# Sparse experts with rings of 12 row slots and 8 weight slots, weights and rows five tiles ahead, two unread products, output by quarters

## The reference

```
    x = x + ctx @ Wo
    m = _layernorm(x, ln2_g, ln2_b)
    xt = m.reshape(-1, Dd)
    probs = jax.nn.softmax(xt @ Wg, axis=-1)
    wts, idx = jax.lax.top_k(probs, K)
    wts = wts / jnp.sum(wts, axis=-1, keepdims=True)
    h1 = jax.nn.gelu(jnp.einsum('td,edf->etf', xt, W1) + b1[:, None, :])
    ye = jnp.einsum('etf,efd->etd', h1, W2) + b2[:, None, :]
    sel = ye[idx, jnp.arange(T)[:, None], :]
    moe_out = jnp.sum(wts[..., None] * sel, axis=1).reshape(Bb, Ss, Dd)
    return x + moe_out
```

## Time and profile before

| what | value |
|---|---|
| median of 3 runs | 2333.95 us |
| the profiled execution | 2350.25 us |
| its span, first to last instruction | 2348.5 us |
| TensorE busy | 1893.6 us (81%) |
| VectorE busy | 1552.4 us (66%) |
| ScalarE busy | 958.3 us (41%) |
| GpSimd busy | 748.9 us (32%) |
| mean granted TensorE clock | 0.904 |
| the expert tiles, first hidden product to last down product | 2201.33 to 2326.83 us |

### The profile page before, as it was taken

How to read it: one execution, slowest core, us unless ns; L and a number is a source line. 1 busy time by engine, 2 the same in 40 slices (tenths; PEclk the granted TensorE clock), 3 DMA queues, 4 the chain that set the end, 5 groups by cost and what they waited for, 6 DMA issues and landing times.

```text
span 2348.5 us, 50210 instructions
## 1 busy us (share of the span) xinstructions
PE 1893.6 (81%) x20232; PEld 1212.9 (52%) x20232; DVE 1552.4 (66%) x3648; ACT 958.3 (41%) x2463; POOL 748.9 (32%) x959
## 2 busy tenths in 40 slices
PE   6678999889898899976787899999999646472864
PEld 3324556555545566435575566666666213252654
DVE  5699985788846754478615766676764899766112
ACT  3436654666536322324124455555553001150232
POOL 2244554555414242134404100000002753325222
PEclk9779999999999999987798999999999877785797
DMA  9000001000071000700341010000000000210465
GB/s 381 7 1 0 1 1 67 4 5 4 4 306 59 3 1 1 293 14 2 111 148 31 19 37 19 19 19 19 10 1 1 0 9 18 102 57 30 144 193 156
DMA packets 56039, 134.80 MB, mean 57 GB/s; under 512 B 13865, under 2 KB 34044, under 8 KB 48128
## 3 DMA queue, kind: packets, MB, share of 16 engines
q1 hardware_dynamic: 52512, 125.48, 15.3%
q0 software_dynamic: 3296, 6.12, 0.8%
HBM read 112.13 MB, written 20.12 MB: 56 GB/s over the span
## 4 chain that ended last, share of the span: by engine, by line
PE 47%; DVE 29%; issue 10%; ACT 7%; DMA 4%; POOL 2%; SPq 1%; POOLq 0%; DVEq 0%; another core or an unknown queue 0%; ACTq 0%
PE PS L2442 3%; PE PS L418 3%; PE PS L362 3%; PE PS L454 3%; PE PS L3105 3%; PE PS L3095 3%; PE PS L3153 2%; DVE arena L1733 2%; DVE arena L248 2%; PE PS L2242 2%; DMA answers<-arena 2%; PE PS L3145 1%; DVE arena L3561 1%; ACT arena L3217 1%; PE PS L3137 1%
## 5 line engine op out<-in xcount | busy, mean ns | idle before, releaser
L315 POOL TENSOR_TENSOR arena<-arena 128x4 f32<-128x4 f32 (+2 forms) x101 | 115.5, 1145 | 852.1 <-DVE arena L259 415.4
L3217 ACT ACTIVATE arena<-PS,arena 128x289 f32<-128x289 f32 x256 | 127.0, 506 | 176.5 <-DVE arena L3322 173.3
L362 PE MATMUL PS<-arena 128*128 128x512 f32 x310 | 168.4, 664 | 5.0 <-DVEq L4058 4.2
L1797 POOL TENSOR_TENSOR arena<-arena 128x128 f32<-128x128 f32 x384 | 140.5, 407 | 52.7 <-PE PS L1660 29.4
L3105 PE MATMUL PS<-arena 128*128 128x289 f32 x512 | 136.1, 409 | 2.3 <-DVE arena L3316 1.7
L1733 DVE RECIPROCAL arena<-PS 128x128 f32<-128x128 f32 x96 | 91.6, 954 | 58.2 <-PE PS L1698 58.0
L1764 ACT COPY arena<-PS 32x128 f32<-32x128 f32 x384 | 99.5, 259 | 52.1 <-PE PS L1674 47.2
L1183 POOL TENSOR_TENSOR arena<-arena 128x512 f32<-128x512 f32 x64 | 85.0, 1328 | 108.7 <-DVE arena L1328 108.7
L382 PE MATMUL PS<-arena 128*128 128x128 f32 x288 | 50.0, 313 | 69.2 <-DVE arena L294 29.4
L3105 PEld LDWEIGHTS PS<-arena 128*128 128x128 f32 x512 | 92.7, 191 | 24.4 <-issue 2.9
L454 PE MATMUL PS<-arena 128*128 128x128 f32 (+4 forms) x576 | 87.6, 298 | 16.8 <-DVE arena L409 4.1
(11 more groups left out here) (411 smaller groups left out, 4844.0 us busy)
## 6 DMA issues: line engine op xcount, KB each, us to landing
arena<-in_ctx SPq DMA_DIRECT2D x48, 1090.0 KB, 7.3
arena<-in_f_w SPq DMA_DIRECT2D x39, 514.0 KB
lists<-arena SPq DMA_DIRECT2D x8, 1040.0 KB, 10.9
arena<-in_f_w SPq DMA_DIRECT2D x32, 256.0 KB
arena<-in_ctx SPq DMA_DIRECT2D x16, 512.0 KB, 4.2
arena<-in_mid SPq DMA_DIRECT2D x1, 3796.5 KB, 11.8
arena<-in_late SPq DMA_DIRECT2D x1, 3204.0 KB, 11.9
arena<-in_w SPq DMA_DIRECT2D x1, 3017.0 KB, 13.5
```

Of the source, the lines that this page charges most:

```text
L315: e.tensor_tensor(x, x, half.broadcast_to(list(x.shape)), ALU.pow).then_inc(*T.done("norm_root", tag))
L362: e.matmul(g.PS[:, b, :], g.C["ident"], g.const_words[:, 0:512], start=True, stop=True)
L1797: k = e.tensor_tensor(dst[:, b], spread(src[:, b, :], [P, HG, S], 1), spread(self.g.C["headmask"], [P, HG, S], 2), ALU.mult)
L3217: e.activation(self.weights(n, k, 0, UL), PS[:, k, 0:UL], ACT.Exp, bias=self.st[:, h, k:k + 1], accum_out=self.st[:, h, 4 + k:5 + k]).then ...
```

## The change

It touches the expert part of the last layer and the output:

- The rows get 12 slots of their own (`SLOTS`), the weights 8 (`RING`). The rows have their own events (`f3_tile`), so that `turn` waits for the rows alone and `hidden` for the weights.
- The weights of five tiles (`LEAD`) are issued before the list is complete, then the rows of these five, then weights and rows of one tile after the other.
- `weights(k)` now waits for `down(k - 8)` and `rows(k)` for the scatter of tile k - 12.
- TensorE turns all four quarters of the gates and then does all four bias products.
- Two unread products are left of 14.
- The output is written in four DMAs, each after its quarter has been added to.

```diff
@@ L3Ffn
-    RING = 6
+    RING, SLOTS, LEAD = 8, 12, 5
@@ __init__
-        self.x = [room.take(self.ROW) for _ in range(self.RING)]
+        self.x = [room.take(self.ROW) for _ in range(self.SLOTS)]
@@
     def loaded(self, k):
+        return f"f3_tile{k % self.SLOTS}", k
+
+    def weighed(self, k):
         return f"f3_weights{k % self.RING}", k
@@ sp
         def rows(k, at):
-            j = k - self.RING
+            j = k - self.SLOTS
             for w in T.due(("f3_rows_out", j), (f"f3_gathered{j % 4}", j)):
                 e.wait_ge(*w)
-            e.dma_start(self.x[k % self.RING], lists[bass.DynSlice(at, 1)].rearrange("a p w -> (a p) w")).then_inc(*T.done(*self.loaded(k), 16))
+            e.dma_start(self.x[k % self.SLOTS], lists[bass.DynSlice(at, 1)].rearrange("a p w -> (a p) w")).then_inc(*T.done(*self.loaded(k), 16))
 
         for w in T.due(("f3_list", 0)):
             e.wait_ge(*w)
-        ahead = [weights(k) for k in range(3)]
+        at = [weights(k) for k in range(self.LEAD)]
         for w in T.due(("f3_scattered", 2 * NT - 1)):
             e.wait_ge(*w)
-        for k in range(self.TILES):
-            rows(k, ahead[k] if k < 3 else weights(k))
+        for k in range(self.LEAD):
+            rows(k, at[k])
+        for k in range(self.LEAD, self.TILES):
+            rows(k, weights(k))
@@ after the loads of the answers
+        out = self.out.rearrange("b s d -> (b s) d")
+        for q in range(NQ):
+            for w in T.due(("f3_final", q)):
+                e.wait_ge(*w)
+            e.dma_start(out[QW * q:QW * q + QW, :].rearrange("(a p) d -> p a d", p=P), quarter(g.X, q)).then_inc(*T.done("out", q, 16))
@@ hidden
-            for w in T.due(free[b], ("f3_sT_dve", k)):
+            for w in T.due(free[b], self.weighed(k), ("f3_sT_dve", k)):
@@
-        idle_pe(e, T, g, free, 6, 14)
+        idle_pe(e, T, g, free, 6, 2)
@@ dve, the last additions
-                e.tensor_tensor(x, x, quarter(self.back[c], q), ALU.add).then_inc(*T.step())
+                e.tensor_tensor(x, x, quarter(self.back[c], q), ALU.add).then_inc(*(T.done("f3_final", q) if c else T.step()))
@@ sync_program
-    e.dma_start(out.rearrange("b s d -> (b s) d").rearrange("(t p) d -> p t d", p=P), g.X).then_inc(*T.done("out", 0, 16))
```

More of the change, by code:

```diff
@@ L70 @@
         "query_out": "lin_out", "located": "lin_out", "select": "cleared", "second_pool": "first",
-        "shifted": "beta", "list": "picked", "count": "picked", "end": "picked", "tiles": "picked", "past": "picked"}
+        "shifted": "beta", "list": "picked", "count": "picked", "end": "picked", "tiles": "picked", "past": "picked", "final": "residual",
+        "weights6": "rows0", "weights7": "rows1", "tile8": "v30", "tile9": "v31", "tile10": "v32", "tile11": "v33"}
+KIND.update({f"tile{k}": f"context{k}" for k in range(8)})
 def work_of(name):
@@ L3657, in weights @@
             e.dma_start(self.w[k % self.RING], t["f3_w"][bass.DynSlice(x, 1)].rearrange("a p f -> (a p) f")).then_inc(
-                *T.done(f"f3_weights{k % self.RING}", (k, 0), 16))
+                *T.done(*self.weighed(k), 16))
             return at
         def rows(k, at):
-            j = k - self.RING
+            j = k - self.SLOTS
             for w in T.due(("f3_rows_out", j), (f"f3_gathered{j % 4}", j)):
                 e.wait_ge(*w)
-            e.dma_start(self.x[k % self.RING], lists[bass.DynSlice(at, 1)].rearrange("a p w -> (a p) w")).then_inc(*T.done(*self.loaded(k), 16))
+            e.dma_start(self.x[k % self.SLOTS], lists[bass.DynSlice(at, 1)].rearrange("a p w -> (a p) w")).then_inc(*T.done(*self.loaded(k), 16))
         for w in T.due(("f3_list", 0)):
             e.wait_ge(*w)
-        ahead = [weights(k) for k in range(3)]
+        at = [weights(k) for k in range(self.LEAD)]
         for w in T.due(("f3_scattered", 2 * NT - 1)):
             e.wait_ge(*w)
-        for k in range(self.TILES):
-            rows(k, ahead[k] if k < 3 else weights(k))
+        for k in range(self.LEAD):
+            rows(k, at[k])
+        for k in range(self.LEAD, self.TILES):
+            rows(k, weights(k))
         for k in range(self.TILES - 4, self.TILES):
@@ L3742, in turn @@
                 e.wait_ge(*w)
-            e.transpose(g.PS[:, b, 0:P], self.x[k % self.RING][:, 0:D], C["ident"]).then_inc(*T.done("f3_turned", k))
+            e.transpose(g.PS[:, b, 0:P], self.x[k % self.SLOTS][:, 0:D], C["ident"]).then_inc(*T.done("f3_turned", k))
             free[b] = ("f3_sT_dve", k)
@@ L3843, in pool @@
         for k in range(self.TILES):
-            at = self.x[k % self.RING][:, D + 1:D + 2].bitcast(mybir.dt.uint32)
+            at = self.x[k % self.SLOTS][:, D + 1:D + 2].bitcast(mybir.dt.uint32)
             for w in T.due(("f3_rows_out", k)):
@@ L4026, in dve @@
                     e.wait_ge(*w)
-                e.tensor_scalar(self.y[j % 4], g.PS[:, 4 + j % 2, 0:D], self.x[j % self.RING][:, D:D + 1], None,
+                e.tensor_scalar(self.y[j % 4], g.PS[:, 4 + j % 2, 0:D], self.x[j % self.SLOTS][:, D:D + 1], None,
                                 ALU.mult).then_inc(*T.done("f3_rows_out", j))
@@ L4074, in pool_program, with sync_program @@
         e.drain().then_inc(*T.done("left_pool", x.ends))
-def sync_program(e, T, layers, g, out):
+def sync_program(e, T, layers, g):
     t = g.t
@@ L4088, in sync_program @@
         e.wait_ge(*w)
-    e.dma_start(out.rearrange("b s d -> (b s) d").rearrange("(t p) d -> p t d", p=P), g.X).then_inc(*T.done("out", 0, 16))
-    for w in T.due(("out", 0), ("in_x", 0), ("in_const", 0), ("in_weights", "first"), ("in_weights", "mid"), ("in_weights", "late"),
+    for w in T.due(*(("out", q) for q in range(NQ)), ("in_x", 0), ("in_const", 0), ("in_weights", "first"), ("in_weights", "mid"), ("in_weights", "late"),
                    ("f2_slots_in", "zero"), ("f2_slots_in", "rows"), *((f"f2_gathered{q}", 4 * q + 3) for q in range(NQ)), ("f2_scattered", NT - 1),
@@ L4099, in program @@
         layers = [x(g) for x in LAYERS]
+        layers[11].out = out
         layers[8].after, layers[9].before = layers[9], layers[8]
@@ L4108, in program @@
         pool_program(dry, View(tally, "pool"), layers)
-        sync_program(dry, View(tally, "sp"), layers, g, out)
+        sync_program(dry, View(tally, "sp"), layers, g)
         tally.dry = False
@@ L4130, in _ @@
         def _(e):
-            sync_program(e, View(tally, "sp"), layers, g, out)
+            sync_program(e, View(tally, "sp"), layers, g)
 def constants():
```

## The result

The changed kernel takes **2273.8 us** (median of 4 runs, 2270.9 to 2277.1), the kernel before 2332.0 us (median of 4). The ratio is 0.9752, with a 95% interval of 0.9728 to 0.9776: 58 us less, between 52 and 63. The forecast was 2269 with a range of 2259 to 2286. Later, on another chip, both were timed again, and the ratio was 0.9709 (0.9680 to 0.9738).

A forecast was written before the change was run, and what follows sets the result against it. The prediction took a closed loop of scatter, row load and products over three tiles as the bound, no engine being busy. Savings of 3.4 + 10.1 + 49.1 + 2.1 = 64.7 us from 2333.95 gave 2269, range 2259 to 2286.

The forecast's parts named there:

- The closed loop of three tiles: Last layer's tiles: each round of scatter, row load and products covers three tiles in 10.7 us, with TensorE waiting.
- loop term: Tiles of the last layer: with the longer rings the loop takes 76.4 us instead of 125.5, 49.1 us less.
- Clock: Start of the tiles: an early full clock saves up to 4 us, a late one loses some 2 us; nothing added.
- The DMA term: Tile loop: DMA engines need 2.14 us a tile, above TensorE's 1.90, so the step was taken as 1.95 us.
- Rival A: Tile loop: the DMA engines become the bound, steps of 2.14 to 2.4 us, time 2276 to 2286; chance 0.28.
- The weights' loop holds six and takes no longer: Weight ring: weights(k) wait for down(k - 8), done in step k - 6, so this loop takes no longer than the rows'.
- The start: Before the first tile: gates and bias products 3.4 us earlier, fewer unread products 10.1 us less, turn(0) at 2187.1.
- The output: End of the kernel: with four output DMAs only the last 256 KB is left, 2.1 us less, bounds 0 and 2.5.
- Rival B: Tile loop: the scatter queues behind the loads, steps of 3.9 us or more, slower at about 2341; chance 0.03.
- C: Tile loop: TensorE loses its clock, half-speed steps of 3.8 us, only the ends gain, 2341 at worst; chance 0.03.
- D: Tile loop: something else closes a loop of three tiles, leaving the ends' 15.6 us, time 2318; chance 0.04.
- The sum: Whole kernel: 3.4 + 10.1 + 49.1 + 2.1 = 64.7 us less, 2.8% of 2350.25, giving 2269.

The follow-up runs named there:

- rings6: The changed kernel with both rings back at 6 slots (RING = 6, SLOTS = 6): 2336.2 us, ratio 0.9940 to the kernel before on that chip.
- slots6: The changed kernel with only the row ring back at 6 slots, weights keeping 8: ratio 0.9908 to the kernel before, tiles 118.8 us.
- idle14: The changed kernel with 14 unread products instead of 2: profiled span 2278.2 us, start and tiles together 129.9 us.
- ringsonly: The changed kernel's rings and loads with the start and output of the kernel before: ratio 0.9751 to the kernel before on chip A.
- changed: The changed kernel, unaltered, run again on chip C: 2274.4 us, ratio 0.9709 to the kernel before.
- after: The changed kernel's profiled execution on the first chip: 2277.1 us, span 2275.1 us, ratio 0.9752 to the kernel before.
- moretraffic: The changed kernel with one more load of 132 KB for each tile from the sixth on: tiles 86.3 us, profiled span 2280.6 us.
- oneout: The changed kernel with one output DMA of 1024 KB instead of four: end 21.4 us, profiled span 2277.9 us.
- ringsonly2: The changed kernel's rings and loads with the start and output of the kernel before, run on chip C: 2286.4 us, ratio 0.9768.
- alternate: The changed kernel with gates and bias products in alternation as before the change: start 48.3 us, tiles 75.0 us, profiled span 2280.1 us.

## Why the prediction was right, step by step

*The closed loop of three tiles* was read rightly, and the runs show it: rings6 brings back 125.5 us, slots6 118.8.

*The size of the loop term* was right for partly wrong reasons, and so in part by luck. Forecast: 76.4 us, from 2.4 + 37 x 1.95 + 1.8. Measured: 76.5, or 76.8 to the end of the last product, as the forecast counts. It comes from 1.90 per step without any lag of the DMA engines, and some 2 us of half clock at the start, a cost that the prediction named under "Clock" and set to nothing. The 0.05 us that it added to each of 37 steps for the DMA engines is as much, and did not come. idle14 and ringsonly, whose tiles begin at full clock, have the 74.5 us that stood there as TensorE's end. The cost isn't steady: `changed`, the same program as after, had 75.2, as its clock rose 3 us earlier.

*The DMA term* was mis-sized. "2.14 us for a tile" divided the busy time of a half-loaded stretch by its tiles. At TensorE's pace the engines took in a tile every 1.90 us at a share of 0.97 (after) or 0.99 (changed), which is at most 1.84 to 1.88 us of busy time. The share in a stretch with gaps doesn't give the time at full load; it was some 15% too high. Rival A therefore fell: TensorE never waited in the tiles. How narrowly is open; the share of 0.99 speaks for little room, but moretraffic, which was to show it, ran at SP's pace. SP was the next bound in the prediction too, at 1.71 us a tile, 0.19 under TensorE's.

The Trainium skill, DMA: Bandwidth & Descriptors, section "Where 436 GB/s comes from", puts the limit from HBM at about 358 GB/s, which the prediction weighed. That was nearer to the 346 of `changed` than the 298 of the row of before; but it isn't a limit on this core, as the context loads moved 422.

*"The weights' loop holds six and takes no longer"* was wrong. The rows of a tile are issued behind its weights, so the loop closes through turn and holds RING - 3 = 5 tiles. It cost nothing only because 8 slots are just enough; with 6 it cost 22 us.

*The start*: 13.5 us forecast (3.4 + 10.1), with nothing late at turn(0). Counted from the first turned gate to the first hidden product it was 12.7 us (30.0 before, 17.3 after) and 12.5 us on chip C (29.8 and 17.4). Something was late after all: the rows, by 1.3 us in the changed kernel, because the last scatter into the lists set them and not TensorE. The prediction's margin of 4.6 us (rows at 2182.5, turn(0) at 2187.1) came out of a disturbed profile. In the profile of before the gates came 7.6 us late (36.7 against 29.1 us after the first scatter) and the last scatter only 2.5 us late (43.5 against 41.0 us), so TensorE seemed to have 5.1 us more than it has. This also puts turn(0) at 2179.3 and not near 2187. Of the two edits the products gave most: idle14's start is 9.1 us longer than oneout's on the same chip. The order of the gates gives 3.4 us where 14 products follow and nothing waits (58.9 for ringsonly2, 55.5 for idle14), 1.9 us of start beside two products, and of that 0 to 1.6 us remain after the tiles (alternate).

The first two profiles differ by 20.3 us at the start. 12.7 us of that are the change, and 7.6 us lie ahead of the gates, where in the last 14 us VectorE idles up to 2.4 us ahead of single small operations in the profile of before, and less than 0.4 us in that of after. It isn't the change's: the same kernel code has starts 11 us apart on chips A and C (69.7 and 58.9 for ringsonly and ringsonly2).

*The output*: 2.1 us forecast, 2.6 to 2.7 measured (ringsonly2 against changed; oneout, from the last addition on). The outputs landed in 2.9 us at the median, where the best row of that size had 3.0.

*Rival B* (the scatter behind the loads, slower) did not come: VectorE never waited for a scatter in the tiles at a DMA share of 0.97. *C* came in a small form, two to three tiles at half clock. *D* fell.

*The sum* was 64.7 us. The runs gave 58 us on the first chip and 67 us on chip C. Profiled execution against profiled execution it was 73 us, and 66 without the 7.6 us just named; the parts account for 65 of that (12.7 + 48.7 + 3.6 for start, tiles and end). The forecast of 2269 took the 64.7 us off the median, and the measured 2273.8 is 5 us above it. Why the medians of the first chip gave some 7 us less than the traces stays open: of the kernel before only one execution was traced.

## What to carry to other kernels

When slots limit a ring, write down for each kind of slot which event frees it, which instruction that event stands behind in its engine's order, and what else its issuing queue holds up; the number of tiles in that closed loop, not the number of slots, sets the pace. A ring for large loads limits the small loads that are issued behind them on the same queue. A DMA share of 0.63 in a stretch with gaps says little about the time at full load; nor do two microseconds with a share of 1.04, whose 270 GB/s gave the prediction 2.4 us for a tile. Take a stretch of many tiles with a share near 1, and ask what paced it. And an experiment that adds traffic adds issues too: compare the step with the time that the issuing engine needs before calling the DMA engines the bound.

## What the runs showed of the hardware that I had not expected

- Divided by their busy share, the DMA engines moved 298 GB/s at a share of 0.63 (before) and 349 GB/s at 0.97 and at 0.99 (after, changed), with the same mix of transfers. Why is not shown.
- SP needs 1.71 us of its own time for a tile's two loads and 2.2 us for three (moretraffic), close to TensorE's 1.90 us: issuing alone can be the bound of a loop of small tiles.
- TensorE ran 52 us without a gap at full clock beside DMA engines at 0.97 to 0.99, 1.90 us a tile as at a share of 0.42 before: the loads of this kernel didn't slow it.
- On one chip VectorE's gates, which came 1.03 us apart before, came up to 5.6 us apart, in all four kernels that ran there. The profile of the kernel before, on another chip, has such waits ahead of its gates. GpSimd's scatters go on beside them, but they do so in the undisturbed executions too. From the timeline of rings6:

```profile
2166.50 0.19 DVE L3968 TENSOR_TENSOR arena<-arena 128x32 f32<-128x32 f32 x1 [3.22 <-issue]
...
2171.40 0.19 DVE L3968 TENSOR_TENSOR arena<-arena 128x32 f32<-128x32 f32 x1 [3.90 <-remote]
```

The operation takes 0.19 us as elsewhere; by the code it waits for nothing but the operations just before it on the same engine, and that wait takes 3 to 4 us. Why was not tried and stays open.
